# First batch of a gated cross-attention and feed-forward block: its rows loaded by two queues, rows of ones copied by DMA, part of an inverse root moved from GpSimd to VectorE

## The chip, the cores and the metric

The kernel runs on one core of one Trainium2 chip. The metric is the device time of one execution in microseconds (us). The time before is the median of three runs. The profile is of one further execution, whose own time is given beside its span.

## The reference, cut to what matters

Eight batches of 256 rows of 256 values. Each batch goes through a layer norm, an attention over the rows of a second input (16 heads of 16 values) and an output projection, then through a second layer norm and a gated feed-forward with quantised weights and activations. The change touches only the first layer norm of batch 0, the loads of batch 0 and a constant that the attention uses.

```python
def _layernorm(x, axis=-1, eps=1e-05):
    m = jnp.mean(x, axis=axis, keepdims=True)
    v = jnp.var(x, axis=axis, keepdims=True)
    return (x - m) / jnp.sqrt(v + eps)

def reference(x, ctx_1024, ...):
    x = x + jnp.tanh(g_xattn[0]) * _L0_xattn_ref(_layernorm(x, axis=-1), ctx_1024, ctx_1024, Wq, Wk, Wv, Wo, bo,
                                                 mask_BxS2_bf1, mask_BxSxS2_bf1)
    x = x + jnp.tanh(g_ffn[0]) * _L0_ffn_ref(_layernorm(x, axis=-1), clip_x, clip_down, w_gate, w_up, w_down)
    return x
```

## The kernel before

The program is written out by hand for each of the five engines and joined by semaphores. It has three stages: projections of the eight batches (about the first 70 us), attention and output projection (to about 185 us), and the feed-forward (to the end). The change is in the first 24 us of the first stage.

**Tiles.** `x_rows` holds all rows of x, 128 partitions by 16 tiles of 256; a batch is two tiles. `ctx_rows` holds two batches of the second input in turn, inside the large buffer `big`. `w_rows` (in `arena`) holds the four projection weights as loaded, `w_t` the turned ones. `k_st` and `q_st`, also in `big`, are the stacked operands of the attention's scores: 96 partitions of rounded parts (`KR` is 96) and two more (`KM` is 98). In `k_st` the two additional partitions hold ones; TensorE reads them from the first `scores_for_exp` (L1451) on.

**Loads.** SyncE (SP) issues most DMAs in one written order (L391 to L411): x of batch 0, Wq, x of batch 1, ctx 1, x 2 and 3, ctx 2, x 4, the gate weight, ctx 3, x 5, the up and down weights, x 6, five small constants, a mask. Then comes the loop over batches at L428, whose first pass issues ctx 4, waits for the parts of batch 0 (L433, L434) and stores them to the scratch tensor `qk_parts` (L435). A load of ctx b waits until TensorE has turned ctx b-2 (`ct_done`, L351); a load of x b waits until x b-2 has landed (L386). ScalarE (ACT) issues ctx 0, Wk, Wv and the full mask (L674 to L677).

**GpSimd (POOL)** fills two identity matrices, `minus_half`, a part of `wd_t` (L490) and the two partitions of ones (L492), each 4096 words of 32 bits long. After that it computes the inverse roots. `rstd` (L496) is six small instructions on 128x2 values: add epsilon (L499), power -0.5 (L500), and a Newton step of four (L501, L502, L504, L506), each waiting for the one before. `project_rstd` calls it for a batch once VectorE's statistics are there (L509).

**VectorE (DVE)** starts with four memsets, then for batch 0 `stats` (L910: two `bn_stats`, two `bn_aggr`), `normalise` (L922: two `tensor_scalar`, after `rstd_done`), `stats` of batch 1, the copy of the turned ctx 0, `normalise` of batch 1 and so on (L971 to L982).

**TensorE (PE)** runs 40 products whose result nobody reads, turns Wq and Wk (L1371, L1372), runs 8 more such products, and then turns the normalised x 0 and ctx 0 (`x_tr`, L1299). ScalarE copies what was turned, and `project` (L1339) multiplies. Between the q and k products of batch 0 and its v product TensorE turns Wv, x 1 and ctx 1 (`second_batch`, L1375).

**Parts.** ScalarE rounds each projected q and k (L702), VectorE subtracts (L940), ScalarE rounds the rest (L711), POOL subtracts again (L516). The three parts go to `qk_parts`. Two batches share the buffer `parts`, so ScalarE's first rounding of batch 2 waits for the store of batch 0 to land (L701: `act.wait_ge(parts_out[p], 16 * j + 16)`).

## Time and profile before

| what | value |
| --- | --- |
| time, median of 3 runs | 249.05 us (247.9 to 249.51) |
| time of the profiled execution | 250.41 us |
| span of that execution | 248.8 us |
| busiest engines over the span | PE 210.6 us (85%), DVE 207.0 us (83%) |
| ACT, POOL | 160.5 us (64%), 133.3 us (54%) |
| mean granted TensorE clock | 0.956 of full speed |

The profiled execution took 1.6 us more than its span, which is what lies around the recorded instructions. Busy shares are means over three stages that have different limits, so they don't tell what a change in the first 24 us is worth.

### The profile page before, as it was taken

To read this page: it belongs to the slowest core of one execution; us is meant where nothing else is said; L and a number is where in the kernel's file an instruction comes from. 1 tells how busy PE (TensorE), PEld (TensorE's weight loads), DVE (VectorE), ACT (ScalarE), POOL (GpSimd) and SP (SyncE) were. 2 spreads that over 40 slices of the span, in tenths; PEclk is the share of its full clock that TensorE was granted. 3 is DMA by queue.
4 is the path that set the end of the run, shared out by engine and by line. 5 is a ranking of instruction groups with operands and counts; after the bars stand their busy time and mean duration, and the time that the engine had idled before them with its cause. 6 is when DMAs were issued, how large, how long until landed. Compare 5 with 4: busy or idle time off the path is not lost.

```text
span 248.8 us, 5433 instructions
## 1 busy us (share of the span) xinstructions
PE 210.6 (85%) x1712; PEld 146.9 (59%) x1712; DVE 207.0 (83%) x417; ACT 160.5 (64%) x296; POOL 133.3 (54%) x235
## 2 busy tenths in 40 slices
PE   6699979979979999999999999989834989846940
PEld 6578868858746676666676767656422433314830
DVE  3388888978898998989999999964977689998990
ACT  2255487466597777787887776767624688838900
POOL 7446567642462343577585948437846444320880
PEclk9999999999999999999999999999995799995996
DMA  6989889999646553555555342000004200000594
GB/s 219 271 224 307 267 259 235 268 242 247 162 128 147 129 137 105 130 128 130 128 114 125 88 120 73 1 4 0 3 1 133 78 0 1 3 1 0 59 148 139
DMA packets 34186, 30.82 MB, mean 124 GB/s; under 512 B 5232, under 2 KB 27760, under 8 KB 34160
## 3 DMA queue, kind: packets, MB, share of 16 engines
q1 hardware_dynamic: 29776, 27.74, 41.5%
q0 software_dynamic: 1360, 1.31, 4.5%
q10 hardware_dynamic: 3024, 1.44, 2.1%
q8 instruction: 14, 0.23, 0.4%
q14 instruction: 12, 0.10, 0.1%
HBM read 20.65 MB, written 9.70 MB: 122 GB/s over the span
## 4 chain that ended last, share of the span: by engine, by line
PE 46%; DVE 18%; ACT 10%; issue 9%; POOL 7%; DMA 4%; SPq 3%; ACTq 0%; POOLq 0%; DVEq 0%
PE bank_o L1468 10%; PE bank_a L1451 9%; PE bank_b L1437 7%; PE bank_a L1345 6%; PE bank_a L1477 5%; ACT arena L795 4%; DMA qk_parts<-arena 3%; DVE h_max L1220 3%; DVE big L1229 2%; DVE arena L1257 2%; PE bank_o L1356 2%; DVE v_all L1263 2%; POOL big L492 1%; PE bank_a L1318 1%; DVE x_rows L1279 1%
## 5 line engine op out<-in xcount | busy, mean ns | idle before, releaser
L935 DVE TENSOR_REDUCE neg_max<-bank_b 128x2 f32<-128x512 f32 x128 | 80.2, 676 | 4.7 <-PE bank_b L1334 3.0
L1451 PE MATMUL bank_a<-big 98*128 98x256 bf16 x256 | 48.9, 273 | 3.9 <-ACT arena L795 2.3
L1437 PE MATMUL bank_b<-big 96*128 96x256 bf16 x224 | 42.7, 272 | 0.2 <-issue 0.2
L795 ACT ACTIVATE arena<-bank_a 128x512 f32<-128x512 f32 x64 | 34.2, 606 | 9.8 <-PE bank_a L1451 9.8
L795 ACT ACTIVATE big<-bank_a 128x512 f32<-128x512 f32 x64 | 33.7, 598 | 9.4 <-PE bank_a L1451 9.2
L1451 PEld LDWEIGHTS bank_a<-big 98*128 98x128 bf16 x256 | 20.9, 97 | 20.4 <-issue 7.7
L1345 PE MATMUL bank_a<-arena,w_t 128*128 128x256 f32 x128 | 30.2, 381 | 1.9 <-DVE resid L940 1.3
L1345 PEld LDWEIGHTS bank_a<-arena,w_t 128*128 128x128 f32 x128 | 23.2, 190 | 5.2 <-issue 2.5
L516 POOL TENSOR_TENSOR arena<-resid,arena 128x512 bf16<-128x512 f32 x16 | 18.2, 1156 | 10.9 <-ACT arena L711 10.9
L1437 PEld LDWEIGHTS bank_b<-big 96*128 96x128 bf16 x224 | 21.2, 97 | 4.2 <-DVE neg_max L935 0.8
L873 ACT ACTIVATE arena<-bank_b,w_scale_x 128x512 f32<-128x512 f32 (+1 forms) x24 | 16.1, 686 | 5.8 <-PE bank_b L1606 1.9
L576 POOL TENSOR_TENSOR x_rows<-x_rows,arena 128x256 f32<-128x256 f32 x14 | 10.2, 726 | 18.0 <-ACT arena L804 18.0
L660 POOL TENSOR_TENSOR big<-arena 128x512 f32<-128x512 f32 x8 | 10.1, 1266 | 17.1 <-ACT arena L877 17.1
L1606 PE MATMUL bank_b<-arena,wgu_t 128*128 128x512 bf16 (+1 forms) x60 | 17.1, 397 | 2.6 <-DVE big L1229 2.6
L702 ACT ACTIVATE arena<-bank_a 128x512 bf16<-128x512 f32 x16 | 9.4, 595 | 13.9 <-PE bank_a L1345 9.6
L1468 PE MATMUL bank_o<-arena,v_cur 128*32 128x256 f32 x256 | 15.7, 382 | 1.1 <-DVE arena L1032 1.1
L1032 DVE STREAM_TRANSPOSE arena<-bank_o 128x512 f32<-128x512 f32 (+1 forms) x17 | 11.6, 681 | 6.0 <-PE bank_o L1468 5.9
L550 POOL CAST max_parts<-max_f 8x256 bf16<-8x256 f32 x16 | 6.2, 387 | 17.5 <-issue 15.1
L1356 PE MATMUL bank_o<-w_t,arena 128*128 128x256 f32 x64 | 15.6, 381 | 0.0
L1468 PE MATMUL bank_o<-big,v_cur 128*32 128x256 f32 x256 | 15.5, 382 | 0.0
L1220 DVE TENSOR_REDUCE h_max<-big 128x1 f32<-128x512 f32 (+1 forms) x24 | 15.2, 670 | 0.0
L1477 PE MATMUL bank_a<-w_t,arena 128*128 128x256 f32 x56 | 14.4, 379 | 0.0
(185 smaller groups left out, 432.9 us busy)
## 6 DMA issues: line engine op xcount, KB each, us to landing
qk_parts<-arena SPq DMA_DIRECT2D x8, 768.0 KB, 5.0
big<-qk_parts SPq DMA_DIRECT2D x32, 192.0 KB, 3.3
big<-qk_parts SPq DMA_DIRECT2D x32, 128.0 KB, 3.3
x_rows<-in_x SPq DMA_DIRECT2D x8, 256.0 KB, 5.3
big<-qk_parts SPq DMA_DIRECT2D x32, 64.0 KB, 3.6
big<-in_ctx SPq DMA_DIRECT2D x7, 256.0 KB, 5.2
out<-x_rows SPq DMA_DIRECT2D x7, 256.0 KB, 3.0
out<-v_all POOLq DMA_DIRECT2D x5, 256.0 KB, 6.3
```

Source lines behind the costliest of these rows:

```text
L516: pool.tensor_tensor(parts[:, p, w, LO[w]], resid[:, p, w], parts[:, p, w, MID[w]], ALU.subtract).then_inc(lo_done, 1)
L795: act.activation(probabilities(h), ring_bank(b, ("exp", h)).rearrange("p (c s) -> p c s", c=QC), ACT.Exp, scale=SCALE).then_inc(exp_done, 1)
L873: act.activation(silu[0:r, c % 3], bank_b[0:r, c % 3], ACT.Silu, scale=w_scale_x[0:r, c:c + 1]).then_inc(silu_done, 1)
L935: dve.tensor_reduce(neg_max[:, p, :, h], bank.rearrange("p (c s) -> p c s", c=QC), axis=AX.X, op=ALU.max, negate=True).then_inc(max_done, 1)
L1220: chain.then(dve.tensor_reduce(h_max[0:r, tile(u)], h_all[0:r, c, bass.ds(n * CW, CW)], axis=AX.X, op=ALU.max, apply_absolute_value=True))
L1345: last = mm(bank_a[:, w, f * S:(f + 1) * S], w_t[:, w, k, f * P:(f + 1) * P], src[:, p, k * S:(k + 1) * S], start=(k == 0), stop=(k == EC ...
L1356: last = mm(bank_o[:, c * E:(c + 1) * E], ctx_t[:, p, k * S + c * P:k * S + (c + 1) * P], w_t[:, 2, k], start=(k == 0), stop=(k == EC - 1))
L1437: done = mm(to, q_st[0:KR, p, h, c * P:(c + 1) * P], k_st[0:KR, p, h], start=True, stop=not masked)
L1451: done = mm(to, k_st[0:KM, p, h, k * P:(k + 1) * P], q_st[0:KM, p, h], start=True, stop=not masked)
L1468: done = mm(bank_o[n * 2 * D:(n + 1) * 2 * D, g % 2 * S:(g % 2 + 1) * S], v_cur[:, p, k, h], probabilities(h)[:, k], start=(k == 0), stop= ...
L1477: done = mm(to[:, 0:E], att_t[:, p, f, c * P:(c + 1) * P], w_t[:, 3, f], start=(f == 0), stop=(f == EC - 1))
L1606: last = mm(to, wgu_t[:, g, k, c * P:c * P + r], xq_t[:, k, bass.ds(n * CW, CW)], start=(k == 0), stop=(k == EC - 1))
```

## The change

Three edits, all at the start of the program.

1. The rows of batch 0 are loaded as two halves of 128 KB, one tile each. SP issues tile 0 as before; ScalarE issues tile 1 as its first DMA, ahead of ctx 0, with a semaphore of its own (`x_half`) that VectorE waits for before the second `bn_stats`.
2. POOL's memset of the ones is gone. VectorE fills `ones_b` (64x128, bf16) with ones after its other memsets, and SP issues two DMAs, each of `ones_b` into one partition of `k_st`, between the loads of the up and of the down weight. TensorE waits for both before the attention.
3. For batch 0 POOL computes only epsilon and the power (`rough_root`), and VectorE does the Newton step in three instructions (`root`). Batches 1 to 7 keep the six instructions on POOL.

```diff
+        rough = sb("rough", [P, 4, QC])
+        ones_b = sb("ones_b", [P // 2, P], BF16)
...
-            x_load(0)
+            sp.dma_start(x_rows[:, 0], x_dram[:, 0]).then_inc(x_in[0], 16)
             w_load(sp, 0, Wq)
...
+            sp.wait_ge(ones_ready, 1)
+            for r in range(KR, KM):
+                sp.dma_start(k_st[r:r + 1].rearrange("r a h s -> r (a h s)").rearrange("r (q e) -> r q e", e=P), ones_b[:]
+                             ).then_inc(ones_rows, 16)
             sp.dma_start(wd_rows[:], w_down.rearrange("(c p) i -> p c i", p=P)).then_inc(ffn_w_in, 16)
...
             pool.wait_ge(pad_zero, 1)
-            pool.memset(k_st[KR:KM].rearrange("r a h s -> r (a h s)").bitcast(mybir.dt.uint32), 0x3F803F80
-                        ).then_inc(ones_rows, 1)
-            pool.wait_ge(ones_rows, 1)
...
+            def rough_root(var):
+
+                alone(pool)
+                chain.step(pool.tensor_scalar(rough[:, 0], var, EPS, None, ALU.add))
+                pool.tensor_tensor(rough[:, 1], rough[:, 0], minus_half[:, 0], ALU.pow).then_inc(rough_done, 1)
...
-            for b in range(3):
+            pool.wait_ge(stats_done, 1)
+            rough_root(mv1[:, 0, :, 1])
+            for b in range(1, 3):
                 project_rstd(b, b % 2)
...
         def _(act):
+            act.dma_start(x_rows[:, 1], x_dram[:, 1]).then_inc(x_half, 16)
             ctx_load(act, 0)
...
+            dve.memset(ones_b[:], 1.0).then_inc(ones_ready, 1)
...
                 for c in range(QC):
+                    if c and isinstance(b, int) and b == 0:
+                        dve.wait_ge(x_half, 16)
                     chain.then(dve.bn_stats(stats1[:, p, c], x_rows[:, tile(b * QC + c)]))
...
+            def root(n, out, done):
+
+                dve.wait_ge(rough_done, n)
+                chain.step(dve.scalar_tensor_tensor(rough[:, 2], rough[:, 1], -0.5, rough[:, 0], ALU.mult, ALU.mult))
+                chain.step(dve.scalar_tensor_tensor(rough[:, 3], rough[:, 2], 1.0, rough[:, 1], ALU.mult, ALU.mult))
+                dve.scalar_tensor_tensor(out, rough[:, 3], 1.5, rough[:, 1], ALU.add, ALU.mult).then_inc(done, 1)
...
             stats(0, 0, 0)
+            root(1, rs1[:, 0], rstd_done)
             normalise(0, 0)
...
-                pe.wait_ge(ones_rows, 1)
+                pe.wait_ge(ones_rows, 32)
```

On POOL, from `minus_half` on, before (`newton` and `rs` are the scratch and the result of the root, `mv` the statistics):

```order
L487 MEMSET minus_half 128x4
L490 MEMSET wd_t 64x256
L492 MEMSET big 2x4096
L499 TENSOR_SCALAR newton<-mv 128x2
L500 TENSOR_TENSOR rs<-newton,minus_half 128x2
L501 TENSOR_TENSOR newton<-newton,rs 128x2
L502 TENSOR_TENSOR newton<-newton,rs 128x2
L504 TENSOR_SCALAR newton<-newton 128x2
L506 TENSOR_TENSOR rs<-rs,newton 128x2
```

and now (`rough` is what VectorE reads):

```order
L494 MEMSET minus_half 128x4
L497 MEMSET wd_t 64x256
L515 TENSOR_SCALAR rough<-mv 128x2
L516 TENSOR_TENSOR rough<-rough,minus_half 128x2
L503 TENSOR_SCALAR newton<-mv 128x2
L504 TENSOR_TENSOR rs<-newton,minus_half 128x2
L505 TENSOR_TENSOR newton<-newton,rs 128x2
```

The memset of `big` and four of the six instructions of the first root are gone from POOL; the six that follow now belong to batch 1. On VectorE, from the last memsets on, now:

```order
L918 MEMSET ones_f 128x128
L919 MEMSET ones_b 64x128
L991 MEMSET w_amax 128x14
L992 MEMSET h_max 128x24
L931 BN_STATS stats<-x_rows 128x6 x2
L935 BN_AGGR mv<-stats 128x2 x2
L941 SCALAR_TENSOR_TENSOR rough<-rough 128x2
L942 SCALAR_TENSOR_TENSOR rough<-rough 128x2
L943 SCALAR_TENSOR_TENSOR rs<-rough 128x2
L948 TENSOR_SCALAR arena<-x_rows,mv,rs 128x256 x2
```

Before, `TENSOR_SCALAR` stood directly behind `BN_AGGR`, and there was no memset of `ones_b`; nothing else changed places. On SP, from the up weight to the store of batch 0's parts, now:

```order
L403 DMA wgu_rows<-in_L_ffn_w_up 128x5x256
L405 DMA wgu_rows<-in_L_ffn_w_up 64x256
L411 DMA big<-ones_b 1x64x128 x2
L413 DMA wd_rows<-in_L_ffn_w_down 128x2x704
L390 DMA x_rows<-in_x 128x2x256
...
L418 DMA pad_u<-in_mask_BxS_bf 16x128
L355 DMA big<-in_ctx 128x2x256
L442 DMA qk_parts<-arena 128x12x256
```

Two issues (one row, x2) are new ahead of the down weight, and so ahead of the store; the rest keeps its order.

## Rows read from the trace of the kernel before

**Rows 1.** The page's head

```profile
span 248.8 us, 5433 instructions
```

**Rows 2.** Chain that ended last, 0 to 40 us: start, us, what

```profile
2.52 3.52 POOL big L492
...
15.88 0.37 SPq L352
...
23.62 7.54 DMA qk_parts<-arena
```

**Rows 3.** Timeline, all engines, 2 to 12 us: start, us, engine, line, what

```profile
2.52 3.51 POOL L492 MEMSET big<- 2x4096 uint32 x1
...
4.64 0.75 DVE L915 BATCH_NORM_STATS2 stats<-x_rows 128x6 f32<-128x256 f32 x2 [2.38 <-DMA x_rows<-in_x]
5.54 0.25 DVE L919 BATCH_NORM_AGGREGATE mv<-stats 128x2 f32<-128x6 f32 x2
...
6.28 0.24 POOL L499 TENSOR_SCALAR newton<-mv 128x2 f32<-128x2 f32 x1 [0.25 <-POOL big L492]
...
6.60 0.72 POOL L500 TENSOR_TENSOR rs<-newton,minus_half 128x2 f32<-128x2 f32 x1
...
6.97 0.61 PE L1368 MATMUL bank_b<-ident_b 128*128 128x128 bf16 x8
7.28 0.67 ACT L686 ACTIVATE w_t<-bank_a 128x256 f32<-128x256 f32 x2
...
8.44 0.20 POOL L506 TENSOR_TENSOR rs<-rs,newton 128x2 f32<-128x2 f32 x1 [0.18 <-POOL newton L504]
8.67 0.74 DVE L925 TENSOR_SCALAR arena<-x_rows,mv,rs 128x256 f32<-128x256 f32 x2 [2.88 <-POOL rs L506]
...
9.46 0.66 PE L1303 MATMUL bank_b<-ident_f,arena 128*128 128x128 f32 x4 [1.88 <-DVE arena L925]
...
10.21 0.25 DVE L919 BATCH_NORM_AGGREGATE mv<-stats 128x2 f32<-128x6 f32 x2
...
10.66 0.23 POOL L499 TENSOR_SCALAR newton<-mv 128x2 f32<-128x2 f32 x1 [2.02 <-DVE mv L919]
```

**Rows 4.** DMA issues of 0 to 1.5 us: size, us from issue to landing

```profile
big<-in_ctx ACTq DMA_DIRECT2D x1, 256.0 KB, 3.4
x_rows<-in_x SPq DMA_DIRECT2D x1, 256.0 KB, 3.6
arena<-in_L_xattn_Wk ACTq DMA_DIRECT2D x1, 256.0 KB, 4.4
```

**Rows 5.** A half us: busy of five engines, then clock, DMA share, GB/s

```profile
3.00:3.50 0.50, 0.50 (x7) 0.50 (x6) 0.00 (x0) 0.50 (x1) 0.50 (x1) 1.00 1.02 358
```

**Rows 6.** Timeline of SP's queue, 0 to 40 us

```profile
16.30 1.38 SPq L387 DMA_DIRECT2D x_rows<-in_x  x1
...
22.14 0.43 SPq L410 DMA_DIRECT2D tg_bo<-in_L_xattn_bo  x1
22.62 0.43 SPq L411 DMA_DIRECT2D pad_u<-in_mask_BxS_bf  x1
...
24.07 3.05 SPq L387 DMA_DIRECT2D x_rows<-in_x  x1
```

**Rows 7.** Timeline of VectorE, 46 to 50 us

```profile
46.88 0.15 DVE L999 TENSOR_SCALAR scal<-scal 128x2 f32<-128x2 f32 x1
47.06 0.17 DVE L1000 RECIPROCAL scal<-scal 128x2 f32<-128x2 f32 x1
...
47.41 0.92 DVE L1003 TENSOR_SCALAR poison<-poison 128x16 f32<-128x16 f32 x1
```

**Rows 8.** Timeline of POOL, 46 to 50 us

```profile
47.15 2.26 POOL L516 TENSOR_TENSOR arena<-resid,arena 128x512 bf16<-128x512 f32 x2
```

**Rows 9.** Timeline of ScalarE, 30 to 32 us

```profile
31.24 1.08 ACT L702 ACTIVATE arena<-bank_a 128x512 bf16<-128x512 f32 x2 [3.69 <-DMA qk_parts<-arena]
```

**Rows 10.** The chain's last pieces of the first stage

```profile
72.97 1.76 DMA big<-max_parts
```

More of the change, by code:

```diff
@@ L250, in flamingo_block @@
         idents, consts, ones_rows = sem("idents"), sem("consts"), sem("ones_rows")
+        x_half, ones_ready, rough_done = sem("x_half"), sem("ones_ready"), sem("rough_done")
         w_tr, w_ready, wo_ordered = sem("w_tr"), sem("w_ready"), sem("wo_ordered")
```

## The prediction

> **What bounds the kernel now.** I read the page first: a span of 248.8 us [rows 1], with no engine that is busy all through, so what an early edit is worth has to be read at its place. The chain of waits came second. Over the first 10 us it runs through POOL: the memset of the ones (from 2.52, 3.52 us) and then the root of batch 0. Later it has two pieces of another kind: from 15.88 SP issues one DMA behind the other, and from 23.62 the store of batch 0's parts is in flight for 7.54 us [rows 2]. The timeline of 2 to 12 us shows the start step by step: x 0 arrives and VectorE begins at 4.64, its statistics end at 5.79 (5.54 + 0.25), POOL begins the root at 6.28 with the memset named as its releaser, ends it at 8.64, VectorE normalises from 8.67 to 9.41, TensorE turns from 9.46 [rows 3]. ScalarE's timeline at 31.24 shows the second narrow place: 3.69 us idle until the store has landed, before it may round batch 2 [rows 9]. So there are two gates in a row: POOL's root sets how early everything up to about 15.9 us runs, and SP's row of issues with the store behind it sets when batch 2 goes on.
>
> **Edit 1, the halves.** Before, x 0 (256 KB on SP's queue) took 3.6 us from issue to landing, and ctx 0, of the same size and issued on the other queue at nearly the same time, 3.4 [rows 4]. They arrived together, so the two queues shared the bandwidth. Now the first thing on each queue is a half of x, so x is complete after 256 KB have moved, not after 512. The DMA engines move 358 GB/s there [rows 5]; 262,144 bytes fewer ahead of it is 0.73 us. I take 0.7. The bounds are 0 (the halves don't land earlier than the whole did) and 0.7; less than 0 is excluded only as far as no byte is added ahead of x.
> The Trainium skill ("DMA: Bandwidth & Descriptors", section Rules for kernel authors) speaks against this edit: transfers from several engines all run on the same 16 DMA engines and interleave, so that spreading them gives no bandwidth and splitting one transfer in two is not worth it. The equal landing times above agree with the interleaving. What I expect from the split is not bandwidth but a change of rank: ctx 0 yields to x 0. If the rule holds for the landing too, the 0.7 falls away, which is the second rival.
> What yields: ctx 0, Wk, Wv and the mask stand one issue and 128 KB further back on ScalarE's queue. Wk landed 4.4 us after an issue at 1.28, at 5.7. Its issue moves back by one (about 0.5 us) and so does its share of the bandwidth (128 KB of its own and as much beside it, 0.7 us), so it lands at about 6.4. TensorE then ends the turning of Wk and its 8 unread products at about 7.5, where it now ends them at 7.58 (6.97 + 0.61), and ScalarE's copy of Wk would end near 7.9 as now (7.28 + 0.67) [rows 3]. That is still ahead of what comes below, by 0.2 us.
>
> **Edit 2, the memset.** It is 3.51 us long but only its tail is on the path. POOL begins the next root 0.20 us after VectorE's statistics (10.46 to 10.66); without the memset it would have begun the first at 5.99, and it began at 6.28 [rows 3]. So 0.29 us goes, not 3.5. With the halves the statistics end 0.7 earlier, at 5.09, and then the memset would have been late by a further 0.7: the two edits need each other. Of VectorE the memset of 64x128 ones asks some tenths at most, inside the idle 2.38 us before 4.64 [rows 3]. If that cover were gone it would cost those tenths. TensorE's wait for the ones stands at the attention, some 40 us later, and costs nothing.
> On SP it adds two issues. Between the up weight and the store SP never waits, so each issue ahead of the store delays it by its full length. Small issues follow each other at 0.48 us (22.14, 22.62) [rows 6]. This one goes to a single partition, a form that the trace doesn't have with 16 KB; I take 0.5 us each, 1.0 in all. The bounds are 0 (the store's flight doesn't depend on when it was issued, or SP's odd long issues shrink) and the longest issues of this queue, 1.38 and 3.05 us each [rows 6].
>
> **Edit 3, the Newton step.** From the end of the power to VectorE's start there are 1.35 us now (7.32 to 8.67) [rows 3]. VectorE's own small dependent steps follow each other at 0.18 us (46.88 to 47.06, 128x2) [rows 7]; three make 0.54, and with the hop from POOL to VectorE of 0.03 us (8.64 to 8.67) [rows 3] and one at the end 0.60. Gain 0.75. The bounds: 0.35 if each step takes the 0.3 us that a stalled handover costs on POOL (6.28 + 0.24 to 6.60), and 0.85 if the last hop costs nothing.
> A rule that could have spoken against it is in the Trainium skill ("GPSIMD Engine Reference", section Specifications): POOL and VectorE share an SBUF interface, and contend where VectorE reads two SBUF inputs, as these three instructions do. The trace shows what an unlucky overlap looks like: a VectorE instruction on 128x16 took 0.92 us at 47.41, while a smaller one just before it took 0.17, and POOL was in a subtraction of 128x512 from 47.15 on [rows 7, 8]. Here POOL is idle while VectorE does the step, since its next root waits for the statistics of batch 1, which stand behind it on VectorE. Were that cover gone, each of the three could take 0.75 us more.
>
> **The sum at the first gate.** 0.7 + 0.29 + 0.75 = 1.74 us. VectorE: statistics end 5.09, power ends about 6.33 (5.29 + 1.04, the 1.04 being 6.28 to 7.32), Newton to 6.92, normalise to 7.67; TensorE turns x 0 from about 7.7 instead of 9.46, just after it is free at 7.5. From there the order is unchanged, and the turning of ctx 1, for which SP waits, ends 1.7 us earlier: ctx 3 is issued at about 14.15 instead of 15.88 [rows 2].
>
> **The sum at the second gate.** SP's row of issues is 7.74 us long (15.88 to 23.62) [rows 2], with no wait that binds. Now it starts 1.74 earlier and is 1.0 longer, so the store is issued 0.74 earlier, at 22.9, and lands 0.74 earlier, at 30.4. ScalarE waits there for 3.69 us already [rows 9], so its other inputs, 1.7 us earlier, only lengthen that wait. What passes is 0.74, not 1.74: 1.0 us of the gain is handed back on SP. From 31.24 on the chain is compute and waits that move with it (the last DMA of the stage, the maxima of batch 0 at 72.97, is released by what runs just before it [rows 10]), so the 0.74 stays to the end. 250.41 - 0.74 = 249.67 us for an execution like the profiled one. That execution was 1.36 above the median of 249.05, so the same step from the median gives 248.3 us.
>
> **The rivals.**
> The price on SP isn't on the path. The issue of x 5 took 1.38 us where its neighbours of that size take about 0.4 to 0.5 [rows 6]; with every load standing elsewhere in time it may be short now, which returns about 0.9 of the 1.0. For it: the stall has no wait behind it, so it belongs to that moment. Against it: a new stall may come as easily. Then 1.65 passes: 247.4 us.
> The halves land no earlier than the whole. Then the first gate moves by 0.29 + 0.75 = 1.04, SP takes 1.0 back, and 0.04 is left: 249.0 us. For it: the equal shares and the rule above. Against it: 256 KB less ahead of x.
> Slower than before: SP's two new issues are long. They write 64 pieces of 256 bytes each into one partition, at a moment when the queues are full. The place is SP between 18 and 20 us, the point from which it decides is 0.87 us per issue (half of 1.74). At 1.38 each, 2.76 in all, the store comes 1.02 later: 250.1 us. At 3.05 each it would be 6.1 - 1.74 = 4.36 later, 253.4 us. For it: two issues of this queue did take that long, one of them behind the store [rows 6]. Against it: small transfers there take 0.43.
>
> **How the numbers follow.** Forecast 248.3: 0.52. No price on SP, 247.4: 0.20. Halves worth nothing, 249.0: 0.16. Long issues, 250.1 and up: 0.12. The range of 246.9 to 250.0 takes in the first three with the spread of the three runs shown, and the near half of the last. What a measurement of this kernel can tell from no change is about 1%, 2.5 us. A gain beyond that is more than all three edits can give (1.74), so it needs luck in the second gate as well: 0.05. A loss beyond it needs issues near 2.1 us each: 0.04. Within: 0.91.
>
> **What would show it.** Right: VectorE's first statistics at about 3.9; POOL's root at about 5.3; three VectorE steps within 0.6 us; TensorE's turning of x 0 at 7.7 and SP's issue of ctx 3 near 14.15; two issues of about 0.5 us; the store at 22.9 and ScalarE's rounding of batch 2 at 30.5, with an idle time before it of about 4.7. Wrong: a turning of x 0 after 8.3 (Wk late, or the halves worth nothing); a store issued after 23.6 (the slow rival) or before 22.2 (the fast one); a rounding of batch 2 that moves by another amount than the store's issue; or a gain at 31 us that is lost again in the two later stages.

## The result, and the profile after

| | before | changed |
| --- | --- | --- |
| median, 22 executions each | 248.58 us (246.81 to 249.83) | 251.44 us (248.8 to 254.97) |
| ratio of the two | | 1.0077 (95% interval 1.0056 to 1.0099) |
| span of the profiled execution | 248.8 us | 247.7 us |
| mean granted TensorE clock (1 is 2.4 GHz throughout) | 0.954 to 0.965 in 142 executions beside the experiments | 0.942 to 0.965 in 22 |
| of these at 0.953 or less | none | 14 |

The changed kernel is slower; 248.3 us, 0.3% faster, was forecast. Here and below the ratio leaves out the executions that lie more than 1.5% above the fastest of their kernel, eight of the 22 here, while the medians keep them, so it is smaller than what the medians say (1.2%). The profiled execution is one of the short ones. It doesn't show the loss (its span is 1.1 us shorter than that of the kernel before), and that is the first thing to learn from this case: the spread has to be explained, not the profile.

Timeline of the changed kernel, 2 to 12 us, to be read beside [rows 3]:

```profile
3.69 0.75 DVE L931 BATCH_NORM_STATS2 stats<-x_rows 128x6 f32<-128x256 f32 x2 [1.29 <-DMA x_rows<-in_x]
4.59 0.25 DVE L935 BATCH_NORM_AGGREGATE mv<-stats 128x2 f32<-128x6 f32 x2
5.05 0.24 POOL L515 TENSOR_SCALAR rough<-mv 128x2 f32<-128x2 f32 x1 [2.59 <-DVE mv L935]
...
6.12 0.16 DVE L941 SCALAR_TENSOR_TENSOR rough<-rough 128x2 f32<-128x2 f32 x1 [1.29 <-POOL rough L516]
...
6.51 0.16 DVE L943 SCALAR_TENSOR_TENSOR rs<-rough 128x2 f32<-128x2 f32 x1
...
6.71 0.73 DVE L948 TENSOR_SCALAR arena<-x_rows,mv,rs 128x256 f32<-128x256 f32 x2
...
7.83 0.66 PE L1319 MATMUL bank_a<-ident_f,arena 128*128 128x128 f32 x4 [1.31 <-DMA arena<-in_L_xattn_Wk]
...
8.76 0.61 PE L1327 MATMUL bank_b<-ident_f,arena 128*128 128x128 f32 x4
```

VectorE starts at 3.69 instead of 4.64, POOL at 5.05 instead of 6.28, the normalising at 6.71 instead of 8.67. But TensorE turns x 0 only at 8.76: it stood idle for 1.31 us for Wk. The issues of the first microseconds say why (size, median us from issue to landing):

```profile
big<-in_ctx ACTq DMA_DIRECT2D x1, 256.0 KB, 4.3
...
arena<-in_L_xattn_Wk ACTq DMA_DIRECT2D x1, 256.0 KB, 6.1
...
x_rows<-in_x ACTq DMA_DIRECT2D x1, 128.0 KB, 2.5
x_rows<-in_x SPq DMA_DIRECT2D x1, 128.0 KB, 2.7
```

Against [rows 4], x 0 lands 0.9 us sooner after its issue, and Wk takes 6.1 us instead of 4.4, from an issue that is 0.4 us later (1.67). While Wk is in flight the DMA engines are not full. The stretch from 5 to 6 us, of the kernel before and then of the changed one (length; busy us and count of PE, PEld, DVE, ACT, POOL; granted clock, DMA share, GB/s):

```profile
5.00:6.00 1.00, 0.81 (x13) 0.63 (x11) 0.65 (x4) 0.00 (x0) 1.00 (x1) 1.00 1.04 349
```

```profile
5.00:6.00 1.00, 0.92 (x14) 0.74 (x13) 0.00 (x0) 0.00 (x0) 0.87 (x2) 1.00 0.66 213
```

SP's queue, beside [rows 6]:

```profile
15.13 0.37 SPq L355 DMA_DIRECT2D big<-in_ctx  x1
...
16.06 1.40 SPq L403 DMA_DIRECT2D wgu_rows<-in_L_ffn_w_up  x1
17.50 0.54 SPq L405 DMA_DIRECT2D wgu_rows<-in_L_ffn_w_up  x1
18.09 1.23 SPq L411 DMA_DIRECT2D big<-ones_b  x2
...
23.93 0.40 SPq L442 DMA_DIRECT2D qk_parts<-arena  x1
24.37 3.29 SPq L390 DMA_DIRECT2D x_rows<-in_x  x1
```

SP starts its row of issues 0.75 us earlier (15.13, not 15.88). The two issues of ones take 1.23 us, the long issue (1.38 us, x 5) is now 1.40 on another one, and the store goes out at 23.93, 0.31 later than before. ScalarE at the second gate, beside [rows 9], and TensorE there, first before and then now:

```profile
31.91 1.08 ACT L715 ACTIVATE arena<-bank_a 128x512 bf16<-128x512 f32 x2 [5.26 <-DMA qk_parts<-arena]
```

```profile
32.71 3.69 PE L1345 MATMUL bank_a<-arena,w_t 128*128 128x256 f32 x16 [1.33 <-DVE resid L940]
```

```profile
33.38 3.69 PE L1369 MATMUL bank_a<-arena,w_t 128*128 128x256 f32 x16 [2.89 <-DVE resid L963]
```

The store was in flight for 7.91 us (31.84 less 23.93), batch 2 goes on at 31.91, 0.67 later, and TensorE's wait before its projections has grown from 1.33 to 2.89 us. One more place has changed, far from every edit. SP's two loads of the second half of the maxima of batch 0, at 72 us, are one row in each kernel. They stand here with TensorE's wait for them, first of before, then of the changed kernel:

```profile
72.28 1.33 SPq L425 DMA_DIRECT2D big<-max_parts  x2
...
74.78 0.39 PE L1451 MATMUL bank_a<-big 98*128 98x256 bf16 x2 [0.95 <-DMA big<-max_parts]
...
75.98 1.93 PE L1468 MATMUL bank_o<-big,v_cur 128*32 128x256 f32 x32
```

```profile
72.92 1.74 SPq L432 DMA_DIRECT2D big<-max_parts  x2
...
75.90 0.39 PE L1475 MATMUL bank_a<-big 98*128 98x256 bf16 x2 [1.43 <-DMA big<-max_parts]
```

TensorE waits for the second of them, 0.95 us before and 1.43 us now. So the changed kernel has three idle gaps of TensorE in its first 80 us, near 7, 31 and 75 us, of which the last two are longer than before.

### The profile page after: what moved, and what is told of

Same layout as the page of the kernel before. It is cut to its first block, busy times and chain, and to the rows that moved or that the text cites. A ratio compares the mean times of both kernels' runs of the same rounds, so it can differ in the third digit from the quotient of the medians.

```text
span 247.7 us, 5430 instructions
## 1 busy us (share of the span) xinstructions
PE 209.0 (84%) x1709; PEld 146.5 (59%) x1712; DVE 207.6 (84%) x421; ACT 160.2 (65%) x296; POOL 129.0 (52%) x230
## 3 DMA queue, kind: packets, MB, share of 16 engines
q0 software_dynamic: 1360, 1.31, 4.3%
## 4 chain that ended last, share of the span: by engine, by line
PE 44%; DVE 21%; ACT 10%; issue 10%; DMA 7%; POOL 6%; SPq 1%; ACTq 0%; POOLq 0%; DVEq 0%
PE bank_o L1492 11%; PE bank_a L1475 9%; PE bank_b L1461 7%; PE bank_a L1501 5%; PE bank_a L1369 4%; ACT arena L808 4%; DMA qk_parts<-arena 3%; DVE h_max L1244 3%; DMA x_rows<-in_x 3%; DVE big L1253 2%; DVE arena L1281 2%; PE bank_o L1380 2%; DVE v_all L1287 2%; DVE arena L948 2%; PE bank_a L1342 1%
## 5 line engine op out<-in xcount | busy, mean ns | idle before, releaser
L1630 PE MATMUL bank_b<-arena,wgu_t 128*128 128x512 bf16 (+1 forms) x57 | 15.8, 385 | 3.1 <-DVE big L1253 2.9
```

Source lines behind the costliest of these rows:

```text
L1630: last = mm(to, wgu_t[:, g, k, c * P:c * P + r], xq_t[:, k, bass.ds(n * CW, CW)], start=(k == 0), stop=(k == EC - 1))
```

## The experiments

Three theories. **Theory S**: the time that the store and SP's issues hand on is all there is. **Theory C**, the first rival: the clock comes back late in the feed-forward, and the later that starts, the more often. **Theory G**, formed on the profile of e4: TensorE's idle gaps let its granted clock fall from 2.4 to 1.2 GHz in some executions, and longer gaps do so in more of them. The count beside each result is of executions with a mean clock of 0.953 or less, against 14 of 22 for the changed kernel (and 8 of 12 when it ran again) and none of 142 for the kernel before, as it ran beside the experiments. One execution more of that kernel, of 361.8 us at a clock of 0.56, is set aside.

### The three edits one by one

**e1_halves**: edit 1 alone.

```diff
-            x_load(0)
+            sp.dma_start(x_rows[:, 0], x_dram[:, 0]).then_inc(x_in[0], 16)
...
+            act.dma_start(x_rows[:, 1], x_dram[:, 1]).then_inc(x_half, 16)
...
```

> Edit 1 alone: the rows of batch 0 in two halves on two queues; POOL keeps the memset and the root. Both theories: x is there at about 3.7 us, but POOL's memset ends at 6.03 and the root starts at 6.3 as before, TensorE turns x 0 at 9.46, though Wk lands near 7.8. SP's row is unchanged, so ScalarE rounds batch 2 at about 31.2. Theory S (SP's issues and the store decide, and what passes there is all there is): time as before, within 0.5 us. Theory C (TensorE's granted clock in the feed-forward comes back late in some executions, and the more often the later the feed-forward starts): start of the feed-forward as before, so no execution above 251 us. Both say no change; a loss here would put the blame on the late Wk.

Measured: 249.22 us beside 248.9, ratio 1.001 (0.9984 to 1.0037), 1 of 12 at a low clock. VectorE began at 3.62, POOL at 6.28 all the same. The halves alone show no gain: the memset still ends later than they land.

**e2_ones**: edit 2 alone.

```diff
-            pool.memset(k_st[KR:KM]...).then_inc(ones_rows, 1)
...
+            sp.wait_ge(ones_ready, 1)
+            for r in range(KR, KM):
+                sp.dma_start(k_st[r:r + 1]..., ones_b[:]).then_inc(ones_rows, 16)
...
```

> Edit 2 alone: ones by two DMAs, no memset on POOL. The root starts 0.28 us earlier; SP's row of issues grows by the 1.23 us that the two took in the changed kernel, so the store is issued at about 24.6 and ScalarE rounds batch 2 near 32.2 (31.24 before, 31.91 with all three edits). Theory S: 1.0 us slower in every execution, 249.6. Theory C: the later start of the feed-forward lets more executions fall to a mean clock of 0.950 or less; some at 252 to 255 us, median 251 or more, at least 1% above before.

Measured: 252.93 us beside 248.9, ratio 1.0164 (1.012 to 1.0207), 4 of 6 at a low clock. Yet in its profile the store was issued at 23.97, 0.35 later than before, and batch 2 went on at 30.8, 0.44 sooner. By theory S this execution would have shown no loss; it was the short one, 249.23 us, of six that reached 254.65. What it does show is a wait of 1.79 us for the maxima, with the pair of issues at 1.74.

**e3_newton**: edit 3 alone.

```diff
             stats(0, 0, 0)
+            root(1, rs1[:, 0], rstd_done)
             normalise(0, 0)
...
```

> Edit 3 alone: Newton's step of batch 0 on VectorE. Root ends 0.75 us earlier, TensorE turns x 0 at about 8.7, nothing is added on SP, Wk is not late; store issued at about 22.9, batch 2 rounded near 30.5. Theory S: 0.7 us faster, 247.9. Theory C: the same, and no execution above 250 us, since nothing is later.

Measured: 249.43 us beside 248.9, ratio 1.0017 (0.9986 to 1.0047), 1 of 12 at a low clock. Not the 0.7 us faster that both theories gave. In its profile TensorE turned x 0 at 8.74 and SP's row of issues began 0.72 earlier (15.16), but the row took 8.34 us with nothing added, where it had taken 7.74, and the store went out at 23.50, 0.12 earlier. Batch 2 went on at 30.35, and the times don't show it.

**e4_ones_late**: all three edits, the ones issued behind the store.

```diff
                 if b == 0:
                     x_load(7)
+                    sp.wait_ge(ones_ready, 1)
+                    for r in range(KR, KM):
+                        sp.dma_start(k_st[r:r + 1]..., ones_b[:]).then_inc(ones_rows, 16)
...
```

> All three edits, but SP issues the two DMAs of ones behind the store of batch 0 and the load of x 7. TensorE turns x 0 at 8.76 as in the changed kernel, the store is issued at about 22.7 instead of 23.93, batch 2 rounded near 30.6. Theory S: 0.6 us faster than before, 248.0. Theory C: the start of the feed-forward is no later than before, so the executions above 251 us vanish: a median at or below that of before. If long executions stay as frequent as with the changed kernel, it is not the delay at the store but something at the start (the late Wk, the split) that brings them.

Measured: 251.9 us beside 248.9, ratio 1.0053 (1.0014 to 1.0092), 9 of 12 at a low clock. Taking the two issues from ahead of the store didn't help, so theory S as the whole story is out, and so is theory C in the form stated (a clock that comes back late in the feed-forward). The profile was of a long execution, of 254.08 us, and gave the lead; in it the store was issued at 24.15 and batch 2 went on at 33.02, not at the 22.7 and 30.6 that I expected, since SP's row began only at 16.71. TensorE's granted clock in 40 slices, from the pages of the kernel before, of the changed kernel and of e4:

```profile
PEclk9999999999999999999999999999995799995996
```

```profile
PEclk9999999999999999999999999999997699995996
```

```profile
PEclk9799988999998899999999999999997699995996
```

The digits to compare are those of the first 90 us (a slice of e4 is 6.3 us). The first two rows have 9 throughout; the third has 7 in its 2nd slice (6 to 13 us), 8 in its 6th and 7th (32 to 44 us), and 8 in its 13th and 14th (76 to 88 us): at the wait for Wk or behind it, behind the wait for the store, and behind the wait for the maxima. The first two rows differ in their 31st slice, 5 against 7, at about 187 to 193 us, where the feed-forward begins. Every kept profile with a mean clock of 0.955 to 0.959 has 5 there, and every one of 0.961 to 0.965 has 6 or 7. So the half clock that all kernels have there is longer in some executions than in others. It is a large part of the spread of the kernel before (86 of its 142 executions at 0.954 to 0.959, 249.5 us on average, and 56 above, 248.5), and it made the changed kernel's profile look good.

### Filling the gaps

**e5_ones_act**: ScalarE issues the ones behind its mask load.

```diff
             act.dma_start(mask_u8[:], ...).then_inc(mask_in, 16)
+            act.wait_ge(ones_ready, 1)
+            for r in range(KR, KM):
+                act.dma_start(k_st[r:r + 1]..., ones_b[:]).then_inc(ones_rows, 16)
...
```

> All three edits, but ScalarE issues the two DMAs of ones at the start, behind its mask load; SP issues what it did before the change. Theory G (TensorE's idle gaps at about 7, 31 and 75 us let its granted clock fall to 1.2 GHz in some executions, and each gap made longer lets it fall in more of them): SP's pair of issues for the maxima at about 72 us takes 1.33 us again (1.74 in all three kernels that had the ones on SP), the third gap is 0.95 us instead of 1.43, the store comes earlier than 23.9; median 249 to 250. Rival O (it is the ones by DMA, or the missing memset, wherever they are issued): median 251.4 or more as with the changed kernel.

Measured: 254.05 us beside 248.94, ratio 1.0195 (1.0144 to 1.0245), 4 of 5 at a low clock. SP's pair took 1.33 us as expected, but the two issues held ScalarE for 6.69 us, and TensorE waited for its copies:

```profile
2.71 0.50 ACTq L686 DMA_DIRECT2D mask_u<-in_mask_BxSxS_bf  x1
3.24 6.69 ACTq L689 DMA_DIRECT2D big<-ones_b  x2
10.04 1.28 ACT L699 ACT_TABLE_LOAD   x1 [10.04 <-issue]
```

```profile
13.14 5.38 PE L1369 MATMUL bank_a<-arena,w_t 128*128 128x256 f32 x16 [3.28 <-ACT w_t L699]
```

The experiment doesn't tell G from its rival, since it broke something else. It does give the price of a fall: behind an idle time of 3.28 us the 16 products took 5.38 us, where they take 3.69 (the granted clock was 0.69 from 13.0 to 18.5 us, and 1.00 before and behind).

**e6_extra_issues**: the kernel before and two more DMAs of the same ones.

```diff
+            sp.wait_ge(ones_ready, 1)
+            sp.wait_ge(ones_rows, 1)
+            for r in range(KR, KM):
+                sp.dma_start(k_st[r:r + 1]..., ones_b[:]).then_inc(ones_again, 16)
             sp.dma_start(wd_rows[:], ...).then_inc(ffn_w_in, 16)
```

> The kernel before, with its memset, roots and loads, and two more DMAs on SP that write the same ones again. Nothing is taken away; only SP's issues are added. Theory G: the pair at 72 us takes 1.74 us, the third gap grows to 1.4 to 1.8 us, the store is issued about 1 us later; median 251.5 to 253, executions at a mean clock of 0.951 and less. Rival O in the form that the missing memset is what counts: as before, 248.9.

Measured: 249.78 us beside 248.94, ratio 1.0022 (0.9993 to 1.0052), none of 11 at a low clock. So two issues ahead of the store cost about 0.8 us of the median (store issued at 24.82, 1.2 later), with an interval that includes no change, and brought no low clocks. The pair at 72 us was 1.33, against what I expected.

**e7_fill_c** and **e8_fill_abc**: the changed kernel, with products that nobody reads queued ahead of TensorE's waits. e7 has the last of these three, e8 all.

```diff
             weight_tr(0)
+            unread(16)
             weight_tr(1)
...
             for b in range(4):
+                if b == 2:
+                    fill(bank_m, 32)
                 project(b, b % 2, b // 2, first=second_batch if b == 0 else None)
...
                     for h in range(H):
+                        if isinstance(b, int) and b == 0 and h == HH:
+                            fill(bank_o, 16)
                         scores_for_exp(b, p, h, known)
```

> The changed kernel, and TensorE runs 16 products of 128x128 that nobody reads in its gap at about 74.5 us, before it waits for the second half of the maxima. Theory G: that gap shrinks from 1.43 to under 0.6 us at no cost, and executions with a clock fall at 80 us vanish; those with falls at 8 and 35 us remain, so a median between, 250 to 250.8. Rival S (only what SP and the store delay counts): 251.4, unchanged.

> As the one before, with products that nobody reads in the other two gaps too: 16 before TensorE turns Wk, 32 before the projections of batch 2. Theory G: no clock fall in the first 80 us in nearly all executions, mean clock 0.956 or above, median 249.3 (what is left is the profiled kernel's own 0.5 us), none above 251. Rival S: 251.4, unchanged, or longer by the products.

Measured: e7 249.7 us, ratio 1.0006 (0.9969 to 1.0044), 2 of 11 at a low clock; e8 249.06, ratio 1.0004 (0.9967 to 1.0041), none of 11, lowest 0.959. Beside 251.44 for the changed kernel, work that computes nothing took 2.4 us off the median. TensorE in e8 at the third gap:

```profile
73.65 1.06 PE L1397 MATMUL bank_o<-ident_b 128*128 128x128 bf16 x16
75.25 0.39 PE L1483 MATMUL bank_a<-big 98*128 98x256 bf16 x2 [0.55 <-DMA big<-max_parts]
```

The falls and the loss went together, so the falls, or the gaps that the products fill, carry the loss. This doesn't settle which gap does.

### Which gap, and why it is long

**f1_before_fills**: the products in the kernel before (16, 16 and 12).

> The kernel before with products that nobody reads in TensorE's three gaps (16 before it turns Wk, 16 before the projections of batch 2, 12 before it waits for the second half of the maxima). Theory G: about half of the executions before have one clock fall more than the rest (mean clock 0.954 to 0.958 against 0.960 to 0.963); if those falls lie in these gaps they vanish, median 248.3, 0.5 us below before. If the half falls come from the last stage, nothing changes: 248.9.

Measured: 248.15 us beside 249.03, ratio 0.9961 (0.9938 to 0.9984), none of 12 at a low clock. The time came out as theory G said, the reason didn't: its executions still lie in two groups, five at 0.958 or 0.959 and seven at 0.960 to 0.964. In its profile SP's long issue of x 5 was gone (0.47 us, not 1.38) and the store went out at 22.88, 0.74 earlier. Where the 0.4% comes from isn't shown.

**f2_gap_c_only** and **g2_gap_c_two**: the kernel before, one or two small DMAs ahead of the two loads of the maxima.

```diff
                 sp.wait_ge(mp_done, 2 * b + half + 1)
+                if isinstance(b, int) and b == 0 and half == 1:
+                    sp.dma_start(scal[:, 23:24], g_xattn.partition_broadcast(P)).then_inc(spare_in, 16)
```

> The kernel before with one more small DMA on SP (a value into an unused column), issued at about 72 us ahead of the two loads of the second half of the maxima of batch 0: nothing but TensorE's third gap grows, by the 0.45 to 0.6 us of one issue, from 0.95 to about 1.4 to 1.6 us. Theory G: the clock falls at about 80 us in a third or more of the executions; median 250.5 or more, and executions at a mean clock of 0.952 and less, which before has none of. Rival S: the 0.5 us and no more, 249.4, clocks as before.

> The kernel before with two small DMAs ahead of the two loads of the maxima, where f2 had one (gap 1.4 us, no falls in 12). The third gap grows to about 1.8 us, as long as in e2, where falls were frequent. Theory G: falls at 80 us in a third or more of the executions (mean clock 0.950 to 0.953), median 250.8 or more. Rival O (something else of the DMAs of ones): no falls, 0.85 us above before, 249.8.

Measured: f2 249.81 us, ratio 1.0019 (0.9996 to 1.0042), none of 12 at a low clock, with a wait of 1.37 us. A miss: 0.4 us more brought no falls and at most about its own length. g2 252.73 us, ratio 1.0139 (1.0096 to 1.0181), 5 of 6 at a low clock. The wait had grown to 2.76 us, more than the 1.8 that I meant, in part as the pair took 1.76 here. The 32 products with v took 3.39 us behind it, where they take 1.93. Stretches of g2 (busy us and count of PE, PEld, DVE, ACT, POOL; then the granted clock, DMA share, GB/s):

```profile
73.00:75.00 2.00, 0.35 (x3) 0.07 (x2) 2.00 (x4) 0.82 (x2) 0.56 (x1) 1.00 0.25 52
75.00:77.00 2.00, 0.89 (x8) 0.78 (x9) 0.53 (x2) 0.46 (x1) 0.00 (x0) 1.00 0.52 154
77.00:79.00 2.00, 2.00 (x20) 0.88 (x21) 1.05 (x2) 1.49 (x4) 0.80 (x2) 0.52 0.80 217
79.00:81.00 2.00, 2.00 (x22) 0.78 (x15) 0.05 (x1) 0.00 (x0) 0.24 (x1) 0.63 0.11 27
81.00:84.00 3.00, 2.84 (x24) 1.90 (x22) 3.00 (x6) 2.76 (x6) 0.62 (x1) 1.00 0.43 107
```

A long enough third gap, with nothing else touched, brings the falls.

**g1_wait_more**: the changed kernel with one more instruction on SP.

```diff
             sp.wait_ge(ones_ready, 1)
+            sp.wait_ge(ones_ready, 1)
```

> The changed kernel with one instruction more on SP: it waits twice, not once, for the (long written) tile of ones. The pair of loads of the maxima at about 72 us took 1.74 us in every kernel that had the ones on SP behind one wait, and 1.33 in the one (e6) that had two waits there. If the place of the code in SP's stream is what lengthens the pair, it takes 1.33 us here, TensorE's third gap is 0.95 to 1.1 us, and with it theory G says median 249.8 (the 0.5 us of the store and a fall now and then), few executions at a mean clock of 0.952 or less. If the pair stays at 1.74, the DMAs of ones themselves lengthen it, and the time is that of the changed kernel, about 251.

Measured: 249.26 us beside 249.13, ratio 0.9984 (0.9956 to 1.0013), 3 of 12 at a low clock; the changed kernel beside it 251.57. A wait that is long fulfilled took 2.3 us off the median. In its profile the store also went out sooner (23.00, where the changed kernel's two profiles have 23.93 and 23.79), so it isn't shown that the wait acts on the third gap alone. SP and TensorE in g1:

```profile
73.21 1.33 SPq L433 DMA_DIRECT2D big<-max_parts  x2
```

```profile
PE bank_a L1476 <- DMA big<-max_parts: 1.0, 1, 1.0
```

**g3_fill_ab**: products in the first two gaps only.

> The changed kernel with unread products in the first two gaps only (e7 had them in the third only, 249.7; e8 in all three, 249.06). Theory G: the falls at 8 and 35 us go, those at 80 us stay; median 250.2, mean clocks of 0.950 to 0.953 in a third of the executions, none of 0.945 or less.

Measured: 249.99 us, ratio 0.9998 (0.9962 to 1.0033), 6 of 12 at 0.951 to 0.953 and none lower, as expected. That these are single falls behind the third gap is argued, since the profile was of an execution without one (0.963).

**g4_after_again**: the changed kernel once more.

> The changed kernel itself once more, beside the three above on one chip: about 251, with executions at a mean clock of 0.945 to 0.952. If the profile falls into a long execution it shows which gaps the clock fell behind: theory G says 8, 35 or 80 us.

Measured: 251.57 us, ratio 1.0075 (1.0042 to 1.0108), 8 of 12 at a low clock. This time the profile was of a long execution, 254.84 us. Stretches around the second and the third gap, columns as above, and TensorE's rows in them:

```profile
31.00:34.00 3.00, 0.11 (x1) 0.14 (x2) 0.95 (x2) 1.31 (x3) 0.68 (x4) 1.00 1.12 357
34.00:36.00 2.00, 2.00 (x6) 1.57 (x7) 2.00 (x4) 2.00 (x5) 1.51 (x2) 0.53 0.86 286
36.00:38.00 2.00, 2.00 (x7) 1.67 (x6) 1.89 (x5) 1.47 (x2) 0.75 (x1) 0.62 0.16 51
38.00:41.00 3.00, 3.00 (x16) 2.59 (x16) 1.52 (x4) 1.18 (x3) 1.90 (x7) 1.00 1.17 298
76.00:78.00 2.00, 0.53 (x6) 0.14 (x4) 2.00 (x5) 0.97 (x2) 0.71 (x1) 1.00 0.12 21
78.00:80.00 2.00, 2.00 (x14) 1.23 (x18) 1.69 (x3) 1.32 (x3) 0.00 (x0) 0.62 0.88 208
80.00:82.00 2.00, 2.00 (x24) 0.89 (x20) 0.14 (x1) 0.76 (x2) 1.05 (x2) 0.52 0.63 179
82.00:85.00 3.00, 2.97 (x35) 1.85 (x28) 2.19 (x5) 1.91 (x4) 0.62 (x1) 1.00 0.13 34
```

```profile
33.89 5.38 PE L1369 MATMUL bank_a<-arena,w_t 128*128 128x256 f32 x16 [2.98 <-DVE resid L963]
```

```profile
77.97 0.39 PE L1475 MATMUL bank_a<-big 98*128 98x256 bf16 x2 [1.47 <-DMA big<-max_parts]
...
79.77 2.97 PE L1492 MATMUL bank_o<-big,v_cur 128*32 128x256 f32 x32
```

The clock is whole up to the wait, half for a few microseconds behind it, and whole again. In the first stretch the projections of batch 2 take 5.38 us, not 3.69; in the second, 32 products with v take 2.97, not 1.93.

### Versions without the falls

**g6_wait_and_fills**: g1 with the products of f1. **g5_newton_fills**: the kernel before with edit 3 and the products of f1.

> The changed kernel with the one wait more on SP (pair at 72 us 1.33 us, store issued at 23.0 in g1) and the unread products in all three gaps (16, 16, 12). Theory G: the falls of g1 at 33 us go too; median 248.0, all mean clocks 0.957 or above; it beats before by 0.4%. Rival: the three edits give nothing once the falls are out, 248.15 as the kernel before with the same products (f1).

> The kernel before with the Newton step of batch 0 on VectorE (e3) and the unread products (f1). Theory G: e3 lost its 0.7 us in falls of the clock (two of 12 executions at 0.949 to 0.955); with the products 247.5, 0.6 us below f1. Rival: the store hides the Newton step's gain, 248.15 as f1.

Measured: g6 248.16 us beside 249.16, ratio 0.9964 (0.9935 to 0.9993). g5 247.82 us, ratio 0.9941 (0.9916 to 0.9967). Neither has an execution below 0.956. Both beat the kernel before, and g5 is the lowest. In g6's profile the path of the prediction came nearly true: Wk was turned at 7.08, x 0 at 7.97, ctx 3 was issued at 14.34, the store at 22.36, and batch 2 went on at 30.15, 0.84 before f1's 30.99. Against f1 (0.9961) neither this nor the Newton step of g5 (0.2%) can be told from nothing: each interval is about 0.3% to either side.

**f3_gaps_and_fills** and **f4_ones_in_gaps**: halves, Newton step, Wk ahead of ctx 0, and POOL's memset cut in two and moved to where POOL waits; f3 has the products too.

```diff
+            rough_root(mv1[:, 0, :, 1])
+            ones(0)
+            project_rstd(1, 1)
+            ones(1)
+            project_rstd(2, 0)
...
```

> A version meant to beat both: the halves and the Newton step of the change, Wk ahead of ctx 0 on ScalarE's queue, the ones by POOL's memset in two pieces that stand where POOL waits for VectorE (no DMA of ones), and the products of f1 in TensorE's gaps. SP's row of issues is that of before and starts 1.5 us earlier, so the store is issued near 22.1 and batch 2 rounded near 29.7. Theory G: 247.4, no execution at a mean clock under 0.956. Rival S: 247.5 too.

> The same without the products in TensorE's gaps. The third gap is 0.95 us as before, the second between 1.3 and 2 us, since everything but the store comes earlier. Theory G: a few executions with a fall at 35 us, median 247.9, 0.5 above the one with the products. Rival S: no difference between the two.

Measured: f3 249.14 us, ratio 0.9993 (0.9965 to 1.002); f4 248.6 us, ratio 0.9991 (0.9961 to 1.002); no low clock in either, one execution of 364.71 us of f3 set aside, as one of the kernel before. Both missed (247.4 and 247.9 were expected), and the products of f3 took nothing off f4, which has no low clocks to take away. TensorE turned x 0 at 8.45 in f4, but x 1 landed only 7.4 us after its issue (6.2 before) and its normalising took 2.29 us beside POOL's second memset (13.09, 1.80 us), so SP's row began at 16.53, 0.65 later than before; the row took 8.18 us and the store went out at 24.71. So here the start was lost on batch 1 and on SP, and in e3 on SP alone.

## Why the prediction was wrong

**The first gate.** The term for the halves had the right mechanism and too small a size (0.95 measured, 0.7 taken, which was also its upper bound). The memset's tail was right (POOL began 0.21 us after the statistics, 5.05 against 4.84), and the Newton step was right: VectorE took 0.59 us from 6.12 to 6.71, 0.62 with the hop from POOL, where I had 0.60. (Its upper bound was written as 0.85; 1.35 less three steps of 0.18 is 0.81.) POOL was idle beside the three steps, so the cover held. In f4 it wasn't, with a memset of 1.80 us from 6.12 on, and the three still took 0.16 us each; what took longer was the normalising behind them, 1.71 us instead of 0.73.

The step that failed is "it lands at about 6.4", the landing of Wk. Its own terms, 5.7 and 0.5 for the issue and 0.7 for the shared bandwidth, make 6.9. That alone would have put the turning of x 0 at about 7.9, by the 0.93 us from TensorE's turning of Wk to that of x 0 (7.83 to 8.76), and not at 7.7. It landed at 7.8, and in the ten profiles with Wk third on ScalarE's queue 5.3 to 6.9 us after its issue, against 4.4. The price of shared bandwidth took the DMA engines to be full; from 5 to 6 us they moved 213 GB/s where they had moved 349. Why isn't shown. The Trainium skill ("DMA: Bandwidth & Descriptors", section Rules for kernel authors) says that spreading DMAs over the issuing engines gives no bandwidth. The trace agrees: x 0 came sooner, and what stood behind it paid. So 0.7 us passed, not 1.74.

**The second gate.** "Two issues of 0.5 us each" was 0.62 each. With the rest of the row SP needed 8.80 us (15.13 to 23.93) where it had needed 7.74, and the store flew 0.37 longer. Instead of 0.74 earlier, batch 2 went on 0.67 later: (-0.75) + 1.06 + 0.37 = 0.68. By the case's own rival (long issues) the point of decision was 0.87 per issue; it fell to 0.35, because the gain at the first gate had shrunk. So that rival named the right direction, but not by its own mechanism, since neither issue was long. The 1.0 us for the two issues was right on average: the row took 7.50 us in the eleven profiles without them in it (6.75 to 8.34) and 8.47 in the nine with them (8.02 to 9.09). But the row's own long issues come and go from one profile to the next, and that is as much as the gain that the edits had to bring through it.

**What I had no term for.** The sentence "from 31.24 on the chain is compute and waits that move with it" is the step that failed most. A wait of TensorE isn't only late work. Behind it the granted clock can be at 1.2 GHz for a few microseconds, and whether it is differs from one execution to the next. "ScalarE waits there for 3.69 us already [rows 9], so its other inputs, 1.7 us earlier, only lengthen that wait" took the longer wait for free: it went from 1.33 to 2.89 us on TensorE, and g4 shows the fall behind it. The same program has mean clocks from 0.942 to 0.965. The Trainium skill ("TensorE: Matmul & The Clock Gate", Part 1) says that the window in which the gate looks at activity is free-running and isn't reset when a kernel starts. If so, the same gap can meet it differently in each execution; the varying clocks agree with that, and no run here shows the window itself. Of the changed kernel's 22 executions the fourteen at a low clock took 252.8 us on average and the other eight 249.9. So most of the loss is in the falls; the rest, about 1.3 us above the 248.58 of the kernel before, is near the 1.12 us by which TensorE goes on later behind the third gap (75.90 against 74.78).

**The third gap.** It accounts for most of the low clocks, but not for most of the time. Filling it alone takes the median from 251.4 to 249.7 and leaves 2 low clocks in 11 (e7), leaving it alone open leaves low clocks in 6 of 12 (g3), and making it long in the kernel before brings them (g2). But g3, with only the first two gaps filled, has a median of 249.99 beside 251.57, so those two are worth about 1.6 us and the third about 1.7. It was 1.43 to 1.79 us long in the profiles of the three kernels with the ones on SP and nothing filled (the changed kernel, e2, e4), because one pair of SP's issues took 1.74 us instead of 1.33. In the kernels whose profile has the pair at 1.33, with nothing filled and nothing else broken (e1, e3, e6, f4, g1), low clocks were 5 of 59. That the pair's length depends on where the code stands in SP's stream is shown in so far as one more wait instruction, which waits for nothing, undoes it (g1), and as the profile of e6, with the same two DMAs and one wait more, doesn't have it. In g2 the pair took 1.76 with no DMA of ones at all. What in the chip does it wasn't tried. Open too is why f2, with a wait of 1.37 us, had no falls while the changed kernel, at 1.43 and 1.47 in two profiles, had many. Their gaps in other executions may be longer; e2's profile has 1.79.

**Right and wrong together.** Without the falls the three edits show no gain (g6 as f1), and perhaps cost 0.9 us if the pair stays long (e8, 249.06, against f1, 248.15, with intervals that overlap and with other counts of products). The Newton step alone may be worth 0.3 (g5 against f1), which isn't more than the scatter. The forecast of 0.74 was not there in the changed kernel. Whether it would be there without the falls stays open, since the intervals of g6 and f1 leave room for 0.7 us.

## What to carry to other kernels

When a change makes something early that then waits, look at what TensorE does meanwhile: a wait that costs nothing by the chain of waits can cost the clock of what comes behind it. Compare the mean granted clock of many executions, not two profiles; a spread that grows is a result. Where such a gap can't be closed, products that nobody reads, sized to end before the wait does, can pay: in the changed kernel they removed the low clocks (e8), in the kernel before they gave 0.4% (f1), where no edit alone showed a gain, and in f3 they gave nothing.

## What the runs showed of the hardware

- A fall of the clock costs 1.7 us on 16 projections behind the second gap (3.69 to 5.38) and 1.0 us on 32 products behind the third (1.93 to 2.97). In g2 the same 32 products took 3.39. Gaps of 1.5 to 3.3 us had falls behind them in some executions.
- In these profiles the issue that follows the largest transfers on a queue is long. Behind the first store of 768 KB the next issue took 3.05 us before and 3.29 in the changed kernel (2.1 in e6, 4.29 in g4); behind the mask of 512 KB two small issues held ScalarE for 6.69 us (e5).
- SP's issues between its load of ctx 3 and that store, the same ones in eleven profiles, took 6.75 to 8.34 us: in seven of the eleven one or two of them took 1.04 to 1.49 us, and the others 0.37 to 0.72.
- The same pair of issues took 1.33 us in the profiles of some programs and 1.74 to 1.76 in those of others, never between. In g1 it went with one wait instruction more, 50 us earlier.
- VectorE's two normalising instructions took 1.71 us while POOL's memset of 2x2048 ran (f4; 1.70 in f3) and 0.73 without it. VectorE's statistics took 0.75 us beside POOL's memset (before) and without it (changed).
- Among the executions of the kernel before and of f3 one each took over 360 us, at a mean clock of 0.56. Nothing here explains them, and they were set aside.
